# Both value products of a pair of units in one piece on TensorE, with the queues of four engines reordered around them

## What is computed

```python
q = (layernorm(x) @ Wq + bq)                 # 512 -> 32 heads x 128
k, v = split(ctx @ Wkv + bkv)                # 8 heads x 128 each
attn = softmax(q k^T / sqrt(128))            # per sequence, 64 x 64
x = x + (attn v) @ Wo + bo
x = x + expert_ffn(layernorm(x))             # router, top 2 of 8, rank 16
```

## Time and profile before

| | |
|---|---|
| median of 3 runs | 1053.06 us (1051.8 to 1053.72) |
| the profiled execution | 1053.65 us, of which its span is 1051.4 us |
| PE busy | 1027.9 us, 98% of the span |
| DVE, POOL, ACT busy | 807.3, 673.9, 555.8 us |
| matmuls recorded | 5409 |

### The profile page before, as it was taken

How to read it: one execution, slowest core, us unless ns; L and a number is a source line. 1 busy time by engine, 2 the same in 40 slices (tenths; PEclk the granted TensorE clock), 3 DMA queues, 4 the chain that set the end, 5 groups by cost and what they waited for, 6 DMA issues and landing times.

```text
span 1051.4 us, 17330 instructions
## 1 busy us (share of the span) xinstructions
PE 1027.9 (98%) x5409; PEld 849.5 (81%) x5409; DVE 807.3 (77%) x1420; ACT 555.8 (53%) x1314; POOL 673.9 (64%) x563
## 2 busy tenths in 40 slices
PE   9999999998999999999999999999999999999996
PEld 7878877777888888888888888888888888887884
DVE  3563355469997988797889878887987797789986
ACT  3032113257766666665567566655765665665420
POOL 1186237768876887678678767876786687584300
PEclk9999999999999999999999999999999999999998
DMA  8746963996383746456372828274655547250013
GB/s 306 215 125 231 322 206 98 377 349 209 132 295 103 261 143 223 157 207 238 126 259 101 319 85 293 101 260 146 221 181 188 207 152 262 99 161 11 2 41 120
DMA packets 85658, 197.99 MB, mean 188 GB/s; under 512 B 10561, under 2 KB 43369, under 8 KB 70385
## 3 DMA queue, kind: packets, MB, share of 16 engines
q1 hardware_dynamic: 83072, 181.73, 50.0%
q10 hardware_dynamic: 2544, 15.73, 3.7%
HBM read 161.78 MB, written 35.65 MB: 188 GB/s over the span
## 4 chain that ended last, share of the span: by engine, by line
PE 75%; DVE 10%; DMA 7%; POOL 4%; issue 1%; ACT 1%; SPq 1%; ACTq 0%; DVEq 0%
PE banks L1683 22%; PE banks L1684 21%; PE banks L1685 21%; PE banks L1829 5%; PE banks L1808 3%; PE banks L1809 2%; DMA values_dram<-parts 2%; DMA raw<-in_L_xattn_Wkv_dram 2%; DMA k_raw<-keys_dram 2%; DVE stats L1238 1%; POOL w_l L600 1%; PE banks L1708 1%; DMA keys_dram<-parts 1%; DMA raw<-in_L_xattn_Wq_dram 1%; DVE xo L1163 1%
## 5 line engine op out<-in xcount | busy, mean ns | idle before, releaser
L1683 PE MATMUL banks<-wo_h,xo 128*128 128x512 f32 x512 | 203.9, 398 | 0.0
L600 POOL TENSOR_TENSOR qT_l<-parts,qT_h 128x512 fp32r<-128x512 f32 x128 | 165.5, 1299 | 56.9 <-ACT qT_h L827 56.8
L1684 PE MATMUL banks<-wo_l,xo 128*128 128x512 f32 x512 | 200.0, 391 | 0.0
L1685 PE MATMUL banks<-wo_h,xo 128*128 128x512 f32 x512 | 199.5, 390 | 0.0
L1683 PE MATMUL banks<-xo,w_h 128*128 128x512 f32 x448 | 176.8, 395 | 1.9 <-DVE parts L1288 1.9
L1684 PE MATMUL banks<-xo,w_h 128*128 128x512 f32 x448 | 174.9, 390 | 0.0
L1685 PE MATMUL banks<-xo,w_l 128*128 128x512 f32 x448 | 174.3, 389 | 0.0
L600 POOL TENSOR_TENSOR xo<-sT,xo 128x512 fp32r<-128x512 f32 (+1 forms) x72 | 102.6, 1425 | 69.3 <-ACT xo L827 69.3
L1163 DVE TENSOR_TENSOR xo<-banks,xo 128x512 fp32r<-128x512 f32 (+1 forms) x156 | 100.8, 664 | 32.2 <-ACT xo L827 31.7
L1683 PEld LDWEIGHTS banks<-wo_h,xo 128*128 128x128 f32 x512 | 96.1, 188 | 23.2
L1685 PEld LDWEIGHTS banks<-wo_h,xo 128*128 128x128 f32 x512 | 96.2, 188 | 21.0
(11 more groups left out here) (145 smaller groups left out, 2270.4 us busy)
## 6 DMA issues: line engine op xcount, KB each, us to landing
xo<-x_dram SPq DMA_DIRECT2D x105, 1024.0 KB, 6.3
x_dram<-xo ACTq DMA_DIRECT2D x14, 1024.0 KB, 12.4
values_dram<-parts SPq DMA_DIRECT2D x64, 128.0 KB, 3.0
keys_dram<-parts SPq DMA_DIRECT2D x32, 256.0 KB, 5.0
k_raw<-keys_dram SPq DMA_DIRECT2D x32, 256.0 KB, 4.9
raw<-in_L_xattn_Wo_dram SPq DMA_DIRECT2D x8, 1024.0 KB, 8.1
v_raw<-values_dram SPq DMA_DIRECT2D x64, 128.0 KB, 3.6
raw<-in_L_xattn_Wkv_dram SPq DMA_DIRECT2D x7, 1024.0 KB, 7.0
```

The source lines that it names most:

```text
L600: return nc.gpsimd.tensor_tensor(dst, src, high_part.bitcast(F32), ALU.subtract)
L1683: mm(dst, stat[0], mov[0], start=start, stop=False)
L1684: mm(dst, stat[0], mov[1], start=False, stop=False)
L1685: return mm(dst, stat[1], mov[0], start=False, stop=stop)
```

## The change

The same work is done; no instruction is added or removed beyond the position of some, and no shape changes. On PE the first value product moves from behind product 6 to behind product 7; the two halves of the second one come one right after the other, behind out 3; product 3 (r = 1) moves from behind scores 00 to behind that value product, and scores 01 behind it. For this the second half of the second value product gets ring slots 2 and 3 (`PV_SLOTS`), the ring slots of `out` are fixed (`OUT_SLOTS`), and the waits follow. On ACT the high parts of the first value product stand together ahead of `swap_sum(2d - 1, 1)`, those of the second one ahead of `swap_sum(2d, 0)` and around `exponents(2d, 0)`. On DVE the low parts of the second value product come behind the fourth output sum, and the second and third weight sum behind them; POOL's `keys_low(2d + 1)` goes behind `normalise(2d, 0)`. The core of the diff, with lines left out:

```diff
+OUT_SLOTS = (2, 3, 1, 0, 0, 1, 2, 3)
+PV_SLOTS = (2, 3)
...
+        def value_bank(d, k, c, i):
+            if d is not None and k == 0 and c == 0:
+                return att[:, i, :]
+            if d is not None and k == 1 and c == 1:
+                return ring[:, PV_SLOTS[i], :]
+            return turn[:, i, :]
...  POOL, duo
                 shift(2 * d, 0)
+                if split: split_q(g + 1, [0], False)
                 query_low(d, "c12", 1)
+                normalise(2 * d, 0)
                 keys_low(2 * d + 1)
+                if split: split_q(g + 1, [2, 1], False)
                 shift(2 * d, 1)
-                normalise(2 * d, 0)
-                if split: split_q(g + 1, [0], False)
-                values_low(2 * d)
                 probs_low(2 * d, 0)
+                if split: split_q(g + 1, [3], False)
+                values_low(2 * d)
                 normalise(2 * d, 1)
...  ACT, duo: from the copy of scores 00 on, as it is after
+                copy_half(2 * d, 0)
+                query_high(d, "c12", 0)
+                query_high(d, "c22", 1)
+                probs_high(2 * d - 1, 1)
+                swap_max(2 * d, 0)
+                if split: split_q(g + 1, [0], False)
+                output_high(2 * d - 1, 0, 0, d, 1)
+                output_high(2 * d - 1, 0, 1, d, 1)
+                exponents(2 * d, 0)
+                output_high(2 * d - 1, 1, 0, d, 1)
+                output_high(2 * d - 1, 1, 1, d, 1)
+                swap_sum(2 * d, 0)
+                query_high(d, "c12", 1)
+                copy_half(2 * d, 1)
+                keys_high(2 * d + 1)
+                if split: split_q(g + 1, [2], False); split_q(g + 1, [1, 3, 5], False)
+                swap_max(2 * d, 1)
+                probs_high(2 * d, 0)
+                exponents(2 * d, 1)
+                copy_half(2 * d + 1, 0)
+                swap_sum(2 * d, 1)
+                values_high(2 * d)
+                if split: split_q(g + 1, [4, 6], False)
+                probs_high(2 * d, 1)
+                if not last: swap_max(2 * d + 1, 0); copy_half(2 * d + 1, 1)
...  DVE, duo: from the first output sum on, as it is after
+                add(0)
+                s_add(2 * d, 0)
+                s_max(2 * d, 0)
+                if split: combine_w(g + 1, 1, False)
+                add(1)
+                s_peak(2 * d, 0)
+                add(2)
+                add(3)
+                output_low(2 * d - 1, 0, 0, d, 1)
+                output_low(2 * d - 1, 0, 1, d, 1)
+                s_sum(2 * d, 0)
+                query_sum(d, p, "c12", 1)
+                output_low(2 * d - 1, 1, 0, d, 1)
+                output_low(2 * d - 1, 1, 1, d, 1)
+                s_inverse(2 * d, 0)
+                if split: combine_w(g + 1, 2, False); combine_w(g + 1, 3, False)
+                s_add(2 * d, 1)
+                s_max(2 * d, 1)
+                p_turn(2 * d, 0)
+                add(4)
+                s_peak(2 * d, 1)
+                if split: combine_w(g + 1, 4, False)
...
+                s_sum(2 * d, 1)
+                s_add(2 * d + 1, 0)
+                s_inverse(2 * d, 1)
+                if not last: add(5); s_max(2 * d + 1, 0); add(6)
+                p_turn(2 * d, 1)
+                if not last: add(7); s_add(2 * d + 1, 1)
...  PE, waits
+                elif (k, r) == (3, 1) and not opening_duo(d):
+                    pe.wait_ge(y_added, d * 8 - 8 + 3)
...
+                elif d is not None and k == 1 and c == 1:
+                    pe.wait_ge(y_added, d * 8 - 8 + 2)
...  PE, duo
                 product(g, p, 6, 1)
-                outputs(2 * d - 2, 0, True)
-                outputs(2 * d - 2, 1, True)
                 product(g, p, 2, 0)
                 product(g, p, 2, 1)
                 product(g, p, 7, 0)
                 product(g, p, 7, 1)
+                outputs(2 * d - 2, 0, d, 0)
+                outputs(2 * d - 2, 1, d, 0)
...
                 out(d, p, 0)
                 scores(d, 0, 0)
-                product(g, p, 3, 1)
                 out(d, p, 1)
-                scores(d, 0, 1)
-                outputs(2 * d - 1, 0)
                 out(d, p, 2)
                 out(d, p, 3)
-                outputs(2 * d - 1, 1)
+                outputs(2 * d - 1, 0, d, 1)
+                outputs(2 * d - 1, 1, d, 1)
+                product(g, p, 3, 1)
+                scores(d, 0, 1)
                 out(d, p, 4)
                 out(d, p, 5)
                 scores(d, 1, 0)
```

More of the change, by code:

```diff
@@ L755, in duo @@
                 shift(2 * d, 0)
-                query_low(d, "c12", 1)
-                keys_low(2 * d + 1)
-                shift(2 * d, 1)
-                normalise(2 * d, 0)
                 if split:
                     split_q(g + 1, [0], False)
+                query_low(d, "c12", 1)
+                normalise(2 * d, 0)
+                keys_low(2 * d + 1)
+                if split:
+                    split_q(g + 1, [2, 1], False)
+                shift(2 * d, 1)
+                probs_low(2 * d, 0)
+                if split:
+                    split_q(g + 1, [3], False)
                 values_low(2 * d)
-                probs_low(2 * d, 0)
                 normalise(2 * d, 1)
                 if split:
-                    split_q(g + 1, [2, 1], False)
+                    split_q(g + 1, [5], False)
                 probs_low(2 * d, 1)
                 if split:
-                    split_q(g + 1, [3], False)
+                    split_q(g + 1, [4], False)
                 if p == 1 and last_group:
@@ L1218, in combine_w @@
                     dve.wait_ge(combined, 4 * g + 1)
+                    if not first:
+                        dve.wait_ge(q_low, 16 * g - 8 + LOW_AT["c12", 0])
                     ins = nc.vector.tensor_tensor(s2, s1, w_block(0, 0), ALU.subtract)
@@ L1223, in combine_w @@
                     dve.wait_ge(combined, 4 * g + 2)
+                    if not first:
+                        dve.wait_ge(q_low, 16 * g - 8 + LOW_AT["c22", 1])
                     ins = nc.vector.tensor_tensor(s4, w_block(0, 1), s2, ALU.subtract)
@@ L1497, in duo @@
                 s_inverse(2 * d - 1, 1)
+                output_low(2 * d - 2, 1, 1, d, 0)
+                query_sum(d, p, "c12", 0)
+                p_turn(2 * d - 1, 1)
                 add(0)
[L1499 to L1501 removed]
                 s_add(2 * d, 0)
[L1503 removed]
                 s_max(2 * d, 0)
[L1505 to L1507 removed]
@@ L1523, in duo @@
                 p_turn(2 * d, 0)
-                if split:
-                    combine_w(g + 1, 3, False)
                 add(4)
-                add(5)
-                if last:
-                    ln_stats("f", 0)
-                s_inverse(2 * d, 1)
+                s_peak(2 * d, 1)
                 if split:
                     combine_w(g + 1, 4, False)
-                s_add(2 * d + 1, 0)
+                if last:
+                    add(5)
+                    for t in range(3):
+                        tile_stats("f", t)
@@ L1534, in duo @@
+                s_sum(2 * d, 1)
+                s_add(2 * d + 1, 0)
+                s_inverse(2 * d, 1)
+                if last:
+                    tile_stats("f", 3)
+                    ln_combine("f", 0)
+                if not last:
+                    add(5)
+                    s_max(2 * d + 1, 0)
+                if not last:
+                    add(6)
                 p_turn(2 * d, 1)
                 if not last:
-                    add(6)
-                    s_max(2 * d + 1, 0)
@@ L1538, in duo @@
                     add(7)
-                if not last:
                     s_add(2 * d + 1, 1)
@@ L1834, in out @@
             def out(d, p, j):
-                if j < 4:
+                if opening_duo(d) and j < 4:
                     pe.wait_ge(summed, d * len(SUMS) + SUM_AT[("c22", "c12")[j // 2], j % 2])
-                else:
-                    pe.wait_ge(y_added, d * 8 - 8 + j - 4 + 1)
-                out_project(2 * d - 2 + j // UT, out_slot(p, j), j % UT)
+                elif opening_duo(d):
+                    pe.wait_ge(y_added, d * 8 - 8 + j - 4 + 1)
+                elif j in (0, 1, 2, 3, 5):
+                    name, r = {0: ("c22", 0), 1: ("c22", 1), 2: ("c21", 1), 3: ("c12", 0), 5: ("c12", 1)}[j]
+                    pe.wait_ge(summed, d * len(SUMS) + SUM_AT[name, r])
+                elif j == 4:
+                    pe.wait_ge(y_added, d * 8 - 8 + 4)
+                else:
+                    pe.wait_ge(o_low, (2 * d - 1) * 4 + 3 + j - 6)
+                out_project(2 * d - 2 + j // UT, out_slot(d, p, j), j % UT)
             def opening():
```

116 lines of the change are left out of this document (42 added, 74 removed), and 2 rows, old and new, of the table VECTOR_TAIL.

## The result

The changed kernel takes 1074.26 us (median of 4 runs, 1073.51 to 1076.48), the kernel before in the same comparison 1053.21 us: a ratio of 1.0203, interval 1.0189 to 1.0217. It is slower by 21 us, where 10 were forecast, and lies above the upper end of 1070. The profiled execution took 1073.9 us with a span of 1071.7, against 1051.4 before.

The account below looks back on a forecast made before the run. PE was taken to bound the kernel. The terms -5.6 + 13.2 (scores and copy, weight-sum duos) + 1.4 (other duos) + 1.0 (tail) gave +10.0 us: 1063.0 us, forecast's own range 1057 to 1069, range to hold the time 1047 to 1070.

Parts of the forecast that it names:

- the bound: Loop from 300 to 960 us: PE, covered for 660.00 of 660 us, alone sets a duo's pace.
- the gain: PE's second value product: one entry to and exit from the 64-row form saved per duo, 0.4 us, 5.6 us over 14.
- the places: Losses expected at scores 10 and 11 behind s_add with weight sums, and at product 2 awaiting the copy of product 1.
- Rival D: On PE, the 0.4 us is the price of the half, not of the switch, and stays: 1068.6 us, 5%.
- Rivals A and B: A: engines keep up, gain whole, 1047.4 us, 25%; B: copy of product 1 late 0.4 us every duo, 1053 us, 9%.
- the steps up to scores 10: Duos with weight sums, DVE and POOL queues: s_add ends at 41.0 or 42.0, scores 10 come 0.9 to 1.1 us late.
- the choice between the branches: DVE's weight sum 3 or POOL's normalisation first; scores 11 then 1.2 to 2.3 us late, taken as 1.75.
- the later branch: POOL's normalisation goes ahead of weight sum 3: s_add ends at 42.0, about 2.3 + 0.45 us per duo, total +13.3 us.
- the copy in the duos behind those without weight sums: ACT's last copy of product 1 comes at 54.1 where product 2 wants it at 53.9.
- the pair: Late start around duos without weight sums: 0.2 us per pair in each of 7 groups, ends 0 and 0.5.
- the size of the tail: End of the last duo: second half's probabilities come later, 0 to 1.5 us more PE wait, taken as 1.0.
- Rival C: Lateness passed on from duos with weight sums, 1 us more in each of 7 groups: 1070 us or above, 8%.

Follow-up runs that it names:

- the gain alone: Kernel before with only the second value product made whole, both halves between out 2 and out 3, no other queue touched: 1044.8 us, ratio 0.9928.
- both causes mended: Changed kernel with swap_max(2d+1, 0) ahead of probs_high(2d, 1) and weight sums 3 and 2 ahead of the fourth output sum: 1054.39 us, ratio 1.0008.

## Why the prediction was right and wrong

**Right: the bound, the gain, the places.** PE set the pace. The gain per duo is 0.43 where 0.4 was forecast, in the first changed duo, in the experiment with the gain alone and, with the other sign, in the one that parts a product. Rival D, that the price is the half's and not the switch's, falls with these. The losses are where the forecast had them: scores 10 and 11 behind `s_add` in the duos with weight sums, and the copy of product 1. The loads that wait for product 3 and the value product's own inputs gave no wait in the loop. Rivals A and B are out: PE waits in every duo but the first, and for two things.

**Right: the steps up to scores 10.** With the 0.78 us taken off that PE had already lost in that duo (it starts at 427.67), `s_inverse` began at 37.0 (forecast 36.7) and its reciprocal ended at 38.5 (38.4), sum 3 ended at 40.6 (40.55), and `s_add` ended at 42.0 (42.0). All six duos with weight sums took this branch.

**Wrong: the choice between the branches.** The forecast worked out both orders of sum 3 and the normalisation, found that the normalisation is ready first, and took the middle, 1.75 us, because its rows show no two such sums in a row. Measured: 1.01 for scores 10, 1.26 for scores 11, 2.27 together, the upper end of its 1.2 to 2.3. The order rule of the Trainium skill, "SBUF — State Buffer", section "Who interferes with whom", gave the later branch; this trace agrees, with the normalisation at 467.04 ahead of the sum that starts at 467.51. The forecast's own times, 38.45 against 38.9, had decided the branch. 6 x 0.52 = 3.1 us. With its own 2.3 for that branch the forecast would have come to some 1066; the larger part of the miss lies in the next three steps.

**Wrong, and the largest: the copy in the duos behind those without weight sums.** Taken at 0.2 for the pair; measured 0.67 (433.81), with the restart 0.78. In the first changed duo, which nothing had delayed, product 2 was wanted 53.86 us from its start (forecast 53.9), but the copy let it start only at 54.53 (forecast 54.1). The chain was right and its sum too short: from the end of `s_add` to the end of the copy it takes 7.64 us (426.12 to 433.76 in the duo from 378.51), where the forecast's 6.85 and 0.54 for the one high part ahead of the copy make 7.39. These 0.25 us are gaps of some 0.03 between the instructions of the chain; the other 0.2 of the 0.43 were lost ahead of it and at its end. Where lead and need are 0.2 us apart, an error of 0.4 is the whole term. Six times 0.78, and 1.16 in the last duo: 5.8 in place of 1.4. The copy in the duos behind those with weight sums was right, 0.46 against 0.45 (behind the last of the six, product 2 waited 0.54 for a low part of the weights).

**Wrong: the restart.** Each pause makes the second matmul behind it 0.10 to 0.11 us late. That stood in no term: three pauses in each of six pairs, 1.9 us.

**Wrong: the size of the tail.** It was forecast 1.0 us longer and is 4.0: from the last matmul of scores 11 to the end of the span it takes 90.4 us (from 981.27), 86.5 before (from 964.93). (The wait of 2.0 us that the forecast quoted for this place was misread: it lies ahead of 300 us, in the opening. The tail's own was another of 1.7, behind a low part on DVE.) The pause ahead of the next value product is 1.24 us longer (the four transposes and the value product begin at 982.39 and 985.97, 3.58 us apart, 2.34 before). Behind it the granted clock fell to 0.50, the lower of its two levels (1.2 GHz). Timeline of PE and busy time by stretch:

```profile
982.39 0.66 PE L1728 MATMUL banks<-ident,raw 128*128 128x128 f32 x4
985.97 0.58 PE L1853 MATMUL banks<-xo,v_h 64*128 64x256 f32 x2 [2.92 <-DVE xo L1174]
...
988.13 0.63 PE L1704 MATMUL banks<-wo_l,xo 128*128 128x512 f32 x1
988.56 0.63 PE L1705 MATMUL banks<-wo_h,xo 128*128 128x512 f32 x1
```

```profile
986.00:992.00 6.00, 6.00 (x23) 4.81 (x24) 5.89 (x10) 3.20 (x9) 0.34 (x1) 0.50 0.01 1
```

PE is covered throughout from 986 to 992, and its matmuls start 0.43 us apart in place of 0.227. But the clock is the smaller part. The run without weight sums has the same code in its tail, its clock stayed at 1.00 there, and its tail takes 89.6 us (973.07 to 1062.7), 3.2 more than before. PE waits in it for DVE's first output sum of the tail (L1650). Busy time by stretch and timeline of PE in that run:

```profile
975.00:988.00 13.00, 8.90 (x52) 7.10 (x53) 12.37 (x23) 8.02 (x20) 3.30 (x3) 1.00 0.05 13
```

```profile
984.45 0.50 PE L1703 MATMUL banks<-wo_h,xo 128*128 128x512 f32 x1 [1.02 <-DVE y L1650]
```

The same sum on DVE, before and in the changed kernel:

```profile
972.40 0.68 DVE L1630 TENSOR_TENSOR y<-banks,y 128x512 f32<-128x512 f32 x1
```

```profile
992.65 0.69 DVE L1650 TENSOR_TENSOR y<-banks,y 128x512 f32<-128x512 f32 x1 [0.64 <-PE banks L1705]
```

It begins 7.47 us behind the last matmul of scores 11 before, and 11.38 in the changed kernel, of which only 0.64 are a wait for PE at the lower clock. The other 10.74 are DVE's: its first low part of the tail begins 1.24 us later (3.26 against 2.02), and a transpose, a maximum and an output sum, 1.93 us, now stand behind that low part and not ahead of it. So about 3.2 of the 4.0 us belong to the order of the change and some 0.8 to the clock. That these three instructions are the cause is read from the timelines; no run moves them.

**The sum, term by term.** Gain -6.0 (forecast -5.6); scores 10 and 11, 6 x 2.27 = 13.6 (10.5); copy behind them, 6 x 0.46 = 2.8 (2.7); copy in the other duos with its restarts 5.8 (1.4); other restarts 1.9 (none); tail 4.0 (1.0). That is 22.1; the loop has another 1.4 us, and the opening's scatter takes 3.2: 20.3, the difference of the spans. In these two executions that scatter was luck for the forecast. Of the 1.4 us, 0.8 lie at the second half of product 7 in five of the duos behind one with weight sums:

```profile
388.42 0.39 PE L1705 MATMUL banks<-xo,w_l 128*128 128x512 f32 x1
388.69 0.50 PE L1703 MATMUL banks<-xo,w_h 128*128 128x512 f32 x1
```

It starts 0.04 us late, and the matmul behind it, at 389.03, another 0.11. Another 0.2 are scores 10 in the first duo with weight sums. Rival C, a lateness passed on, has at most these 1.4 us. The range failed by the same route: its upper end added the upper bounds, but the bound of the pair, 0.5, was itself below the 0.78 measured, that of the tail, 1.5, was below its 4.0, and the restart had no bound at all.

**Open.** Why the clock falls behind a pause in one run and not in another (below); and whether a better order of DVE in the tail would give its 3.2 us back.

## To carry to other kernels

When an engine is covered to the last per cent, a switch saved on it is worth its price only as long as nothing else comes late by it: the same 0.43 us per duo came in whole with two calls moved on PE, and was lost four times over when scores 01 were moved as well and three queues were reordered around them. Where a forecast has worked out which of two waiting instructions is ready first, take that branch and not the mean; and where a lead is as small as the gaps between the instructions of its chain, measure the chain end to end in a timeline instead of adding up durations. Add to each new pause the price of the start behind it, and look for a swap or copy that waits in its queue behind something it doesn't need.

## What the runs showed of the hardware

- In the loop of the changed kernel, a matmul behind a pause of PE is followed by one that is 0.10 to 0.11 us late (470.53 to 470.75 is 0.22 where scores start 0.12 apart; 433.81 to 434.15 is 0.34 in place of 0.227), even where the pause is only 0.04 us (388.69 to 389.03).
- A DVE sum of two SBUF operands that met a running low part or normalisation on POOL ended behind it at both lengths here: 1.23 us in place of 0.17 with 16 columns, 1.54 in place of 0.69 with 512. The short one ends 0.03 us behind POOL's instruction (466.68 against 466.65), the long one 0.54 (469.05 against 468.51). Two such sums in a row didn't keep a waiting POOL instruction out (467.04, drawn with 1.47 us in place of 1.05).
- The granted clock fell to 0.50 in the tail behind the pause around the four transposes, for about 6.8 us in the changed kernel and in the one with both causes mended (pauses of 3.58 and 3.60 us), and for about 3.4 us in the run with the swap ahead, the one with short sums, the one with the tail's order changed and the one that parts a product (3.57, 3.57, 2.26 and 2.34 us). It stayed at 1.00 in the kernel before and in the run of the gain alone (2.34 and 2.33 us), and in the one without weight sums (3.56). The length of the pause alone doesn't tell, and what does was not found.
- What the lower clock cost depends on what else PE would have waited for: in the run that parts a product, whose tail has the order of before, 3.4 us of it made the tail 1.5 us longer (88.0 against 86.5); in the changed kernel 6.8 us of it cost about 0.8 (90.4 against 89.6), as DVE's output sum would have held PE anyway.
